# Attention's first group: loaded head by head, its projection products spread between its maxima, and a shorter lead of the maxima that grows back over two groups

## The reference, cut to what matters

```
x = x + 0.5 * moe(layernorm(x))     # mixture of 8 experts, 2 per token, capacity limited
x = x + attention(layernorm(x))     # 16 heads of 16 numbers, causal
x = x + 0.5 * moe(layernorm(x))
```

```
Q, K, V = x Wq' + bq, x Wk' + bk, x Wv' + bv
scores  = Q K' / 4  +  lambda * (tanh(Q) J) tanh(K)'      # J: 16 x 16 of this head
probs   = softmax(scores, causal)
out     = (probs V) Wo' + bo
```

## Time and profile before

| | us |
|---|---|
| median of 3 runs (1586.29 to 1590.52) | 1590.41 |
| profiled execution | 1584.54 |
| its span | 1582.8 |
| TensorE busy in the span | 1436.4 (91%) |
| VectorE busy | 1021.7 (65%) |
| ScalarE busy | 712.4 (45%) |
| GpSimd busy | 682.5 (43%) |
| mean granted TensorE clock | 0.95 |

### The profile page before, as it was taken

One profiled execution on the slowest core, in us unless ns is written; L12 is line 12 of the kernel. 1 busy time (PEld: TensorE's weight loads), 2 busy tenths in 40 slices (PEclk: granted clock), 3 DMA queues, 4 the chain that ended last, 5 costly groups with the idle time before them and its releaser, 6 DMA issues. The chain is left out here.

```text
span 1582.8 us, 25424 instructions
## 1 busy us (share of the span) xinstructions
PE 1436.4 (91%) x8840; PEld 1082.3 (68%) x8840; DVE 1021.7 (65%) x2599; ACT 712.4 (45%) x1116; POOL 682.5 (43%) x650
## 2 busy tenths in 40 slices
PE   4699999999665899999999999999986999999998
PEld 3589988989544455555555555555564888989997
DVE  7755665555374777777777777788358666565554
ACT  5333333333232156656566666566564333333332
POOL 1375556554523433333333331333413556556643
PEclk9799999999867699999999999999987999999999
DMA  9454443442467936666566668573055444344422
GB/s 306 130 108 97 95 92 64 87 99 28 85 196 221 267 92 163 176 161 175 160 177 163 164 161 235 157 215 118 28 180 156 112 96 80 74 96 100 91 38 25
DMA packets 125191, 208.60 MB, mean 132 GB/s; under 512 B 24280, under 2 KB 86232, under 8 KB 122008
## 3 DMA queue, kind: packets, MB, share of 16 engines
q1 hardware_dynamic: 88456, 160.06, 35.3%
q0 software_dynamic: 30720, 38.46, 14.8%
q10 hardware_dynamic: 5904, 8.66, 1.9%
HBM read 126.36 MB, written 84.64 MB: 133 GB/s over the span
## 5 line engine op out<-in xcount | busy, mean ns | idle before, releaser
L2006 ACT ACTIVATE a_wts<-a_s_psum 128x1024 f32<-128x1024 f32 (+1 forms) x384 | 300.9, 809 | 180.8 <-PE a_s_psum L2123 178.7
L1882 DVE CUSTOM_DVE_ANT_0 a_m_psum<-a_m_psum,mask 128x128 f32<-128x128 f32 (+3 forms) x512 | 249.0, 502 | 129.5 <-PE a_m_psum L2098 122.7
L2098 PE MATMUL a_m_psum<-a_kp,a_qp 96*128 96x512 f32 (+2 forms) x768 | 287.9, 408 | 26.3 <-DVE a_parts L1882 10.2
L2098 PEld LDWEIGHTS a_m_psum<-a_kp,a_qp 96*128 96x128 f32 x768 | 147.8, 195 | 146.4 <-DVE a_parts L1882 62.1
L1830 POOL TENSOR_SCALAR_AFFINE_SELECT a_wts<-a_wts 128x512 f32<-128x512 f32 x128 | 78.2, 634 | 332.3 <-ACT a_wts L2006 332.3
L1032 ACT ACTIVATE e_act_a<-e_a_psum 128x512 f32<-128x512 f32 (+1 forms) x192 | 101.2, 527 | 259.5 <-PE e_a_psum L1109 259.5
L2123 PE MATMUL a_s_psum<-a_qp,a_kp 97*128 97x512 f32 (+2 forms) x768 | 210.1, 356 | 0.4 <-ACT a_wts L2006 0.2
L243 POOL DMA_INDIRECT e_slots<-normalized,e_token x160 | 167.0, 1044 | 81.7 <-issue 47.5
L949 DVE TENSOR_TENSOR e_hid<-e_act_a,e_g_psum 128x512 f32<-128x512 f32 (+1 forms) x192 | 114.6, 597 | 132.5 <-PE e_g_psum L1109 128.1
L1128 PE MATMUL e_o_psum<-e_w_hi,e_h_hi 128*128 128x256 f32 x640 | 183.2, 286 | 0.0
L1885 DVE TENSOR_REDUCE a_parts<-a_m_psum 128x1 f32<-128x512 f32 x256 | 176.4, 689 | 9.2 <-PE a_m_psum L2098 6.6
(11 more groups left out here) (269 smaller groups left out, 2690.7 us busy)
## 6 DMA issues: line engine op xcount, KB each, us to landing
packs<-x_res SPq DMA_DIRECT2D x48, 512.0 KB, 5.9
e_w_raw<-in_W_in SPq DMA_DIRECT2D x16, 1024.0 KB, 6.4
a_qp<-packs SPq DMA_DIRECT2D x16, 1024.0 KB, 8.0
a_kp<-packs SPq DMA_DIRECT2D x16, 1024.0 KB, 14.0
e_w_raw<-in_W_out SPq DMA_DIRECT2D x16, 512.0 KB, 8.3
normalized<-r_xn SPq DMA_DIRECT2D x16, 512.0 KB, 4.6
x_res<-sums SPq DMA_DIRECT2D x8, 1024.0 KB, 11.4
packs<-q_pack SPq DMA_DIRECT2D x16, 512.0 KB, 5.8
```

The source lines that it names most:

```text
L1882: nc.vector.tensor_tensor_reduce(products, products, c["mask"][:, QC - width:], 1.0, MASKED, ALU.add, ALU.max, top).then_inc(max_read, 1)
L2006: nc.scalar.activation(wts[(u * NS + s) % 2][:, j, 0:w], s_ps[q % 2][:, 0:w], ACT.Exp).then_inc(weighed, 1)
L2098: nc.tensor.matmul(m_ps[bank((n, h, z))][:, 0:stream], qp[n % NB][0:PACK, h, qt * P:(qt + 1) * P], kp[n % NB][0:PACK, h, part * QC:part * ...
```

## The change

Three things are changed, and SyncE's list with them.

1. Group 0 is loaded by heads: head 0, then head 1, then heads 2 and 3, four DMAs each, with a semaphore each; its values follow with a semaphore of their own. TensorE waits for a head's semaphore before that head's first unit, and for the values before the first `mix`. Group 1 is loaded right behind, before the tokens of half 3 and the packs of half 2.
2. `IN_FIRST` spreads the products: only x0 and x1 stand ahead of the first unit; y00 before entry 2, y01 before 4, v0 before 8, v1 before 11, t0 before 15, v2 before 18, v3 before 21, y10 before 25, y11 before 28, t1 before 42 (entries are units and turns).
3. The lead: 52 units stand before the first score, not 60 (`FIRST_LEAD` 4), and one more is added in every sixth step, until the lead is 12 again at step 48, the beginning of group 2.

```diff
+FIRST_HEADS = ((0, 1), (1, 2), (2, GH))
+HEAD_LOADS = 4
+
+def load_heads_of(eng, group, packs, heads, sem):
+    qp, kp, _ = group
+    h0, h1 = heads
+    rows = packs.rearrange("n a (r j) c -> n (a r) j c", j=GH)[0, :, h0:h1, :]
+    for t, to, at, n in ((qp, 0, 0, 4 * HD), (kp, 0, 4 * HD, 2 * HD), (qp, 4 * HD, 0, 2 * HD), (kp, 2 * HD, 4 * HD, 4 * HD)):
+        eng.dma_start(t[to:to + n, h0:h1, :].bitcast(F32), rows[at:at + n, :, :]).then_inc(sem, 16)
...
-        SHARE = [2] * (NS * GH)
...
-        assert len(SHARE) == Q and sum(SHARE) == PER_GROUP
+        SHARE = PER_GROUP // Q
+        FIRST_LEAD, EXTRA_AT = LAG, 6
+
+        def taken(g, q):
+            step = g * Q + q
+            return PER_GROUP + step * SHARE + min(LEAD, FIRST_LEAD + step // EXTRA_AT)
...
-            first = PER_GROUP * (g + 1) + LEAD + sum(SHARE[:q])
             at = lambda units: after_units[min(units, len(after_units) - 1)]
-            return EVENTS[at(first):at(first + SHARE[q])]
+            return EVENTS[at(taken(g, q)):at(taken(g, q + 1))]
...
-        IN_FIRST = {0: (("x", 0), ("x", 1), ("y", 0, 0), ("y", 0, 1), ("v", 0), ("v", 1), ("v", 2), ("v", 3), ("t", 0)),
-                    8: (("y", 1, 0),), 12: (("y", 1, 1),), 40: (("t", 1),)}
+        IN_FIRST = {0: (("x", 0), ("x", 1)), 2: (("y", 0, 0),), 4: (("y", 0, 1),), 8: (("v", 0),), 11: (("v", 1),), 15: (("t", 0),),
+                    18: (("v", 2),), 21: (("v", 3),), 25: (("y", 1, 0),), 28: (("y", 1, 1),), 42: (("t", 1),)}
...
-            for at, event in enumerate(EVENTS[:after_units[PER_GROUP + LEAD]]):
+            for at, event in enumerate(EVENTS[:after_units[taken(0, 0)]]):
...
-                load_group(nc.sync, tiles[0], packs, v_dram, 0, loaded[0])
+                for heads, landed in zip(FIRST_HEADS, heads_in):
+                    load_heads_of(sp, tiles[0], packs, heads, landed)
+                sp.dma_start(vg[0][:].rearrange("p t h c -> p (t h c)"), v_dram[0, :, :, :].rearrange("p t c -> p (t c)")).then_inc(values_in, 16)
+                load_group(nc.sync, tiles[1], packs, v_dram, 1, loaded[1])
                 next_half(FIRST_LATER + 1)
                 packs_out(FIRST_LATER, 0)
-                load_group(nc.sync, tiles[1], packs, v_dram, 1, loaded[1])
                 values_out(FIRST_LATER)
...
-                    if (h, z) == (0, 0):
-                        pe.wait_ge(loaded[n % NB], (n // NB + 1) * NL * 16)
+                    first_of = [heads[0] for heads in FIRST_HEADS]
+                    if n == 0 and z == 0 and h in first_of:
+                        pe.wait_ge(heads_in[first_of.index(h)], HEAD_LOADS * 16)
+                    if n and (h, z) == (0, 0):
+                        pe.wait_ge(loaded[n % NB], (n // NB + (1 if n % NB else 0)) * NL * 16)
...
+                    if (g, s) == (0, 0):
+                        pe.wait_ge(values_in, 16)
```

More of the change, by code:

```diff
@@ L1574, in attend @@
         loaded = [group_in] + kit.sems("a_loaded", "1 2")
+        heads_in, values_in = kit.sems("a_heads_in", "0 1 2"), kit.sem("a_values_in")
         row_in = kit.sems("a_row_in", "0 1 2 3")
```

## The result

The changed kernel took 1601.58 us, the median of 4 runs (1601.34 to 1603.25), against 1588.35 for the kernel before beside it (4 runs): the ratio is 1.0094, with a 95% interval of 1.0077 to 1.0111. So it is slower by some 15 us by the ratio and 13 by the two medians, outside the range of the forecast. The profiled span grew from 1582.8 to 1599.8 us, by 17.0.

The account below looks back on a forecast made before the run. TensorE was taken to bound the loop; the ramp waited for group 0's load, then VectorE set its pace. 1.4 us gained in the ramp and 1.6 given back make +0.2, 1590.6 us; range 1580 to 1598.

Parts of the forecast that it names:

- The shorter lead: Groups 0 and 1: eight units left out of the ramp come back, costing 1.6 us, bounds 0 and 4.8.
- The removed wait: Ramp start: head 0 lands at 502.6 (bounds 501.5 and 505.3), so maxima may begin 10.7 us earlier.
- The ramp behind it: From head 0's landing to the first score: 52.9 us, summed as 17.8 + 12 + 12 + 8.9 + 2.2.
- the first `a_tops`: Sign in the ramp: it would come at 520 to 523.
- the end of head 2: Sign in the ramp: 22 to 27 us behind the first `a_tops`.
- the first score: Sign at the ramp's end: at 553 to 558; forecast 555.5, 1.4 us earlier than before.
- the end of head 1: Sign in the ramp: 11 to 13 us behind the first `a_tops`.
- groups 0 and 1: Sign in the loop: these groups longer by 1.5 to 2 us.
- The moved loads and new waits: Later packs, group 2's load, extra SyncE issues and the values' wait: costed at nothing, each under 0.5 us, either sign.
- Rival 1: Ramp: clock stays at 0.5 through heads 0 to 2, ramp 58.9 us, first score +4.6, total 1596.6 us; chance 0.24.
- rows late: Loop: at lead 4, scores of group 0 or 1 wait for a head's row, some 3 us, 1593.6 us; chance 0.06.
- rival 2: Ramp: products find VectorE busy, so the earlier start is kept; 13.0 us net gain, 1577.4 us; chance 0.20.

Follow-up runs that it names:

- e15: Changed kernel with lead 4 up to step 16 of group 0, then one unit more in each of eight steps: ratio 1.0071, 1599 us.
- e14: Loads by heads with the product list of before; lead 4 up to step 16 of group 0, then one unit more in each of eight steps: ratio 1.0048.
- e10: Kernel before with lead 4 in groups 0 and 1, one more every two groups, up to 9: 1674.34 us.
- e6: Changed kernel with the product list of before and a constant lead of 7 units: 4.0% slower than the kernel before.
- e5: Changed kernel with the product list of before and a constant lead of 8 units: 1.34% (21 us) slower than the kernel before.
- e9: Kernel before with lead 8 in groups 0 and 1, one more every two groups, 12 from group 8 on: 1605.67 us.
- e1: Changed kernel with lead 12 from the start, loads by heads and spread products kept: ratio 1.0056 to the kernel before.
- e3: Changed kernel with lead 12 and the product list of before, so only the loads by heads differ from the kernel before: ratio 1.0005.
- e11: Changed kernel with the lead growing from 4 to 12 in the first eight steps of group 0: 0.54% (8.6 us) less than the changed kernel.
- after: The changed kernel itself, against the kernel before: 1601.58 us, ratio 1.0094.
- e2: Kernel before with only the changed kernel's shorter, growing lead: 90.1 us from first to fifth copy, 78.8 before; total not given.
- e7: Kernel before with lead 4, then one more in each of the first eight steps: no measurable cost, ramp 3.7 us shorter; total not given.
- e12: Loads by heads with the product list of before, lead growing from 4 to 12 in the first eight steps: ratio 0.9996 to the kernel before.
- e4: Changed kernel with a lead of 4 units to the end: 1800.74 us, beside 1611.06 for the kernel before.

## Why the prediction was wrong

**The step that failed is "The shorter lead":** +1.6 us, bounded by 0 and 4.8. It measured 16.2 between the two profiles. The direction was right (the eight units do come back in the loop), the size was off by ten, in four terms:

1. The price of a unit. I took 405 columns at a product's rate, 0.19 us. e15 and e14 measured 0.66 for one more unit between others at clock 1.00: 5.3 us for the eight and not 1.6. The busy time alone, 0.36, is twice what I took, and a bank has to be free as well. The upper bound, 8 x 0.6, was 0.5 short of that and stood on VectorE setting the pace; with VectorE busy for 19.2 of 26.1 us a unit still waits for the one bank that it needs.
2. A lead has a price by itself, even with no unit added. I had no such term. From the second half to the fourth the changed kernel passes leads 6 and 7, 8 and 9, 10 and 11. From the same halves of e10 and e6, of e5 and e9, and of e9 (mean of both leads, over the time at lead 12) that is 1.7, 0.8 and 1.1 us: 3.6 of the 7.8 us of these halves. The other 4.2 are about six of the eight units, which at e15's price are 4.0.
3. Half clock at the start of group 2: 3.6 us. I looked for the clock in the ramp only and took the loop's 0.95 to 1.0 as given.
4. The first half, +4.7 us. Here two causes overlap: half clock outlasts the ramp in nearly all variants (25.2 us in e1, without any short lead, for the 21.7 of before), and two units are added. e1 against before gives some 0.37 us per us of half clock (13.1 us of it in e1, 3.5 before, from the lengths and mean clocks of this half). The same rate gives e3 its 23.3 us to 0.1 and leaves 0.6 for lead 8 in e9. By it the 9.6 us of half clock in the changed kernel are 2.2 us, an estimate, and the rest is units and leads 4 and 5. No run separates them.

3.6 + 4.2 + 3.6 + 4.7 is 16.1. The first three rest on halves that repeat to 0.1 us where the clock stays full; the fourth compares single profiles of a half that took 21.7 us before and 23.3 in e3 with the same work, and is the least certain.

**What held.** The removed wait: landing at 503.7, 1.1 us later than forecast (502.6); 0.4 of that is the first issue, at 498.03, and that the rest is the other heads' DMAs, issued right behind, is only argued. TensorE's wait ended on it, as forecast. The ramp behind it: 52.9 forecast, 54.3 measured (head 0 16.3 for 17.8, head 1 13.2 for 12, head 2 13.3 for 12, head 3 9.4 for 8.9). It was my largest sum, and its error is 1.4 us, but that is in part luck: the errors of the heads have both signs (-1.5, 1.2, 1.3, 0.5), and with the same list it took 55.2 us in e11 and 57.7 in e15. Of the signs that I had named, the first `a_tops` (520.0), the end of head 2 (26.6 us behind it) and the first score came within their bounds, the end of head 1 (13.2 for 11 to 13) just missed, and groups 0 and 1 missed widely. The moved loads and new waits cost nothing: no unit or score waits for a load but the first unit.

**The clock in the ramp.** The stages of heads 0, 1 and 2 in the changed kernel, columns as in the earlier trace rows:

```profile
503.70:520.00 16.30, 10.89 (x37) 6.96 (x37) 7.78 (x23) 3.92 (x5) 7.23 (x8) 0.81 1.05 251
520.00:533.20 13.20, 11.04 (x29) 7.34 (x30) 7.72 (x23) 0.91 (x2) 1.89 (x2) 0.50 0.98 337
533.20:546.60 13.40, 11.34 (x28) 6.60 (x26) 6.99 (x23) 2.67 (x5) 7.26 (x8) 0.63 0.96 236
```

The granted clock was 0.81, 0.50 and 0.63. I had 1.0 from y01 to somewhere in head 1 and again from about y11. In steps of 2 us it was 1.0 from 510 to 520, but 0.50 from the start of head 1 at 520 on to 540 and again from 544: my forecast was a little too slow for head 0 and too fast for heads 1 and 2. (My reading of the ramp before was off by 0.3 us at either end: the means of 0.77 and 0.79 put the rise at 522.9 and the fall at 533.2.) My figures for the two levels hold better than my choice between them. The stage of head 0 in e15, at half clock throughout:

```profile
504.50:524.10 19.60, 14.71 (x37) 9.90 (x37) 7.74 (x22) 3.92 (x5) 7.20 (x8) 0.50 1.03 242
```

I had 20.0 us for head 0 at half clock, and 13.4 for head 1, which took 13.2 in the changed kernel, e11 and e15 alike, each time at 0.50. The Trainium skill's page "TensorE: Matmul & The Clock Gate", section "A second HAM failure mode: psum-queue depth-cycling", says that small idle times from going round the PSUM banks between groups of matmuls make the clock swing and the throughput fall. I weighed it for the ramp. The trace agrees that the clock swings where TensorE idles between maximum units (0.50 in head 1 with TensorE busy for 11.04 of 13.2 us) and at the turn to group 2. It does not bear out that the idle time alone decides: at 4.53 us of 5.7 the clock stayed in e9, at 5.12 it fell in e15.

**The rivals.** None was it. Rival 1 had half the ramp's clock right: it was to decide from a ramp of 52.7 us on, and 54.3 were measured, but not the 58.9 of half clock throughout, so the first score comes 1.05 us later and not 4.6. Its total of 1596.6 was nearest, by another place than the loss; "rows late" had the right place, the loop, with a mechanism that needs a lead of 4 at a group's turn; rival 2, the faster one, was far off, since the spread products cost the ramp 8.7 us (e1 less e3). What was missing is a rival that prices the new leads themselves. The profile hinted at it: VectorE is busy for 28.7 of 39.5 us and TensorE for 37, and both take turns on the same banks; such a loop may have a best lead, and of those measured lead 12 is it.

By the ratios, the whole 0.94% is about 0.55% for growing over two groups and not in eight steps (after less e11, e2 less e7; each difference is uncertain by 0.2 to 0.3%), some 0.4% for the spread products (e11 less e12), and nothing that can be told for the loads and a fast growth (e3, e7, e12).

## What to carry to other kernels

Where two engines hand banks to each other with little time to spare, how far one runs ahead of the other is a parameter with a price for each value, and passing slowly through the values pays them all: change it in few steps, or step over the dear ones. Price an added unit by its own row plus the wait for its bank, not by its columns. And a shorter prologue is not a gain before the loop behind it has been read half group by half group, clock included.

## What the runs showed of the hardware that was not expected

- A 256 KB store from ScalarE's queue took 14.1 us to land in e4 beside a 3.3 MB load from SyncE's queue, and a 4 KB row behind it kept TensorE waiting for 10.6 us. Two queues did not keep the small transfer from the large one. The kernel before shows the same: 2.0 to 2.2 us for the stores at 579, 619 and 658, and 12.8 and 13.9 for those at 600 and 637, each issued within 0.7 us of a load. But there a head's row leaves ahead of the load (592.7 for a load at 599.7).
- The order of work within a stretch repeats to 0.1 us between kernels once the clock is full (18.9, 18.5, 20.5, 20.8 us for a half in nearly every variant at lead 12), and a stretch of half clock at the turn of a group, costing 1.5 to 4 us, comes and goes: in e15 the stretch ahead of it reads alike at group 2, where it does not come, and at group 8, where it does.
- Leads 4, 8 and 12 are cheap, and 5, 6, 7, 9 and 11 dear, by 1.2 to 2.3 us in twelve steps with the same instructions. Why 6 belongs to the dear ones and 10 hardly does, these runs do not show.
